# Layer 2's routed experts: the weights of a pair of experts laid side by side, loaded by three DMAs in place of six

## The reference, cut to what matters

```
g = jnp.einsum('ech,ehi->eci', buf, w_gate)
u = jnp.einsum('ech,ehi->eci', buf, w_up)
y = jnp.einsum('eci,eih->ech', jax.nn.silu(g) * u, w_down)
out_slots = y[flat_i, slot] * (flat_w * valid)[:, None]
```

## Time and profile before

| | us |
|---|---|
| median of 3 runs | 2361.2 |
| lowest and highest of them | 2356.06, 2362.68 |
| the profiled execution's time | 2355.61 |
| span of its trace, first to last instruction | 2353.9 |
| TensorE busy | 1996.5 (85%) |
| VectorE, GpSimd, ScalarE busy | 1291.5, 868.5, 757.3 |
| routed experts of layer 2, from about 1914 us on | some 440 |

### The profile page before, as it was taken

One profiled execution on the slowest core, in us unless ns is written; L12 is line 12 of the kernel. 1 busy time (PEld: TensorE's weight loads), 2 busy tenths in 40 slices (PEclk: granted clock), 3 DMA queues, 4 the chain that ended last, 5 costly groups with the idle time before them and its releaser, 6 DMA issues. The chain is left out here.

```text
span 2353.9 us, 39125 instructions
## 1 busy us (share of the span) xinstructions
PE 1996.5 (85%) x11898; PEld 1415.1 (60%) x11899; DVE 1291.5 (55%) x3013; ACT 757.3 (32%) x2192; POOL 868.5 (37%) x840
## 2 busy tenths in 40 slices
PE   1988888895699999569999999999999878878876
PEld 1666666663477777447777777777777643333332
DVE  5888888874244444336666777767666622111221
ACT  2323333322222222155544555554555211111110
POOL 5455665633343343142433333333343231211111
PEclk9998999997799999759999999999999989888898
DMA  6422222231133333422211111112222359999996
GB/s 214 153 84 89 88 73 89 86 120 41 45 100 103 104 97 101 145 71 83 78 64 65 64 65 63 65 64 77 96 82 80 105 188 351 357 356 351 361 358 183
DMA packets 129946, 315.30 MB, mean 134 GB/s; under 512 B 33346, under 2 KB 41538, under 8 KB 121604
## 3 DMA queue, kind: packets, MB, share of 16 engines
q1 hardware_dynamic: 102772, 260.64, 31.6%
q0 software_dynamic: 26880, 52.68, 7.8%
q10 hardware_dynamic: 144, 0.03, 0.0%
HBM read 253.13 MB, written 62.33 MB: 134 GB/s over the span
## 5 line engine op out<-in xcount | busy, mean ns | idle before, releaser
L1566 ACT ACTIVATE attn_pr<-attn_score_ps,attn_nmax 128x128 f32<-128x128 f32 x496 | 201.9, 419 | 198.7 <-DVE attn_nmax L1719 198.7
L1677 POOL DMA_INDIRECT list<-attn_pair,attn_pos x192 | 192.2, 1001 | 72.1 <-issue 61.1
L328 PE MATMUL attn_ffn_ps<-attn_xnT_high,attn_wgu_high 128*128 128x256 f32 x704 | 209.1, 297 | 9.2 <-DVE attn_hT_low L1811 8.2
L328 PE MATMUL attn_ffn_ps<-attn_xnT_low,attn_wgu_high 128*128 128x256 f32 x704 | 200.2, 284 | 0.0
L328 PE MATMUL attn_ffn_ps<-attn_xnT_high,attn_wgu_low 128*128 128x256 f32 x704 | 200.0, 284 | 0.0
L300 POOL TENSOR_SCALAR attn_norm_var_eps<-attn_norm_mean_var 128x2 f32<-128x2 f32 x32 | 7.9, 248 | 469.3 <-DVE attn_norm_mean_var L294 469.2
L1964 POOL DMA_INDIRECT out<-routed_ym,routed_place x32 | 50.2, 1569 | 340.9 <-DVE routed_ym L2127 267.4
L527 PE MATMUL wkv_ffn_ps<-wkv_xnT,wkv_wg 128*128 128x256 f32 x512 | 147.6, 439 | 24.9 <-DVE wkv_x L842 23.8
L1719 DVE TENSOR_REDUCE attn_nmax<-attn_score_ps 128x2 f32<-128x256 f32 x248 | 126.3, 551 | 60.2 <-PE attn_score_ps L1408 59.3
L1011 POOL DMA_INDIRECT y<-routed_ys,first_ffn_pair x72 | 74.0, 1028 | 230.3 <-DVE routed_ys L1161 230.3
L328 PE MATMUL routed_gu_ps<-routed_wgu_high,routed_xT_high 128*128 x288 | 126.0, 438 | 36.1 <-POOL first_ffn_wgu_low L968 36.1
(11 more groups left out here) (292 smaller groups left out, 5076.2 us busy)
## 6 DMA issues: line engine op xcount, KB each, us to landing
second_ffn_room<-in_w_gu SPq DMA_DIRECT2D x32, 1408.0 KB, 26.9
routed_wgu_a<-in_w_gu SPq DMA_DIRECT2D x16, 1408.0 KB, 24.4
routed_wgu_b<-in_w_gu SPq DMA_DIRECT2D x16, 1408.0 KB, 27.5
wkv_x<-in_x SPq DMA_DIRECT2D x32, 512.0 KB, 4.1
second_ffn_room<-y SPq DMA_DIRECT2D x32, 512.0 KB, 5.4
second_ffn_room<-in_w_down SPq DMA_DIRECT2D x32, 512.0 KB, 24.4
wkv_vT<-in_ctxT SPq DMA_DIRECT2D x16, 512.0 KB, 4.2
xn<-wkv_xn SPq DMA_DIRECT2D x16, 512.0 KB, 2.8
```

Source lines behind the costliest of these rows:

```text
L328: ins = nc.tensor.matmul(out, a[i], b[j], start=start and n == 0, stop=stop and n == 2)
L1566: nc.scalar.activation(pr[u % 2][:, a, j:2 * j + 1, :].rearrange("p k t -> p (k t)"), score_ps[:, a, KEYS[j]], ACT.Exp, bias=nmax[u % 2][: ...
L1677: nc.gpsimd.indirect_dma_start(io["list1"], bass.IndirectOffsetOnAxis(ap=pos[b.s][:, j, k:k + 1], axis=0), pair[b.s][:, j, k, :], None, bo ...
```

## The change

The weights of a pair are laid side by side in HBM, partition by partition, and in SBUF. A partition's share of gate and up of both experts is one run of 22,528 bytes, loaded by one DMA. Down is split by partitions and not by blocks: partitions 0 to 95 hold three rows of each expert, one run of 12,288 bytes, and partitions 96 to 127 hold two of each, 8,192 bytes in HBM that go to two places of 4,096 bytes in SBUF. That makes two DMAs, so a pair has three in place of six. The slots have the same size and number; SP's waits stand where they stood, and TensorE's counts are halved. The diff, without its repeated index changes:

```
-        wgu += [[m.sb(f"wgu_{s}_{z}", [P, 2, KC, H1]) for z in "ab"] for s in range(EARLY1, SLOTS1)]
-        wdn += [[m.sb(f"wdn_{s}_{z}", [P, HW, C]) for z in "ab"] for s in range(EARLY1, SLOTS1)]
+        wgu += [m.sb(f"wgu_{s}", [P, 2, 2, KC, H1])[:] for s in range(EARLY1, SLOTS1)]
+        wdn += [m.sb(f"wdn_{s}", [P, 2, HW, C])[:] for s in range(EARLY1, SLOTS1)]
...
-                        c.late.load_up(sp, io, 2 * q.i, slot, wgu[slot])
+                        c.late.load_up(sp, io, q.i, slot, wgu[slot])
...
-                    pe.wait_ge(up_in[q.s % SLOTS1], 32 * uses(q))
+                    pe.wait_ge(up_in[q.s % SLOTS1], 16 * uses(q))
...
-                    pe.wait_ge(down_in[q.s % SLOTS1], 64 * uses(q))
+                    pe.wait_ge(down_in[q.s % SLOTS1], 32 * uses(q))
...
-    def load_up(self, sp, io, e, slot, wgu):
-        for z in range(2):
-            sp.dma_start(wgu[z][:].rearrange("p z k n -> p (z k n)"), of(io, "w_gu1", e + z)).then_inc(self.up_in[slot], 16)
-
-    def load_down(self, sp, io, e, slot, wdn):
+        return self.at(s * self.SLOT + 4 * KC * H1, 2, -(-H1 // P), C)
+
+    def load_up(self, sp, io, q, slot, wgu):
+        sp.dma_start(wgu.rearrange("p e z k n -> p (e z k n)"), of(io, "w_gu1", q)).then_inc(self.up_in[slot], 16)
+
+    def load_down(self, sp, io, q, slot, wdn):
         full = H1 // P
-        for z in range(2):
-            sp.dma_start(wdn[z][:, 0:full, :].rearrange("p k n -> p (k n)"), of(io, "w_down1", e + z)).then_inc(self.down_in[slot], 16)
-            sp.dma_start(wdn[z][0:H1 - full * P, full, :], of(io, "w_down1_rest", e + z)).then_inc(self.down_in[slot], 16)
+        rest = H1 - full * P
+        sp.dma_start(wdn[0:rest].rearrange("p e k n -> p (e k n)"), of(io, "w_down1", q)).then_inc(self.down_in[slot], 16)
+        sp.dma_start(wdn[rest:, :, 0:full, :], of(io, "w_down1_rest", q).rearrange("p (e k n) -> p e k n", e=2, n=C)
+                     ).then_inc(self.down_in[slot], 16)
...
+    def by_pair(a):
+        return np.ascontiguousarray(a.reshape(PAIRS1, 2, a.shape[1], -1).swapaxes(1, 2)).reshape(PAIRS1, a.shape[1], -1)
+
...
+        "w_gu1": by_pair(np.stack([by_partition(i["L1_ffn_w_gate"]), by_partition(i["L1_ffn_w_up"])], axis=2)),
+        "w_down1": by_pair(np.concatenate([down1[:, :rest1], i["L1_ffn_w_down"][:, H1 // P * P:][:, :, None]], axis=2)),
+        "w_down1_rest": by_pair(down1[:, rest1:]),
```

More of the change, by code:

```diff
@@ L1347, in weights_ahead @@
                 def weights_ahead(s):
-                    c.late.load_up(sp, io, 2 * s, s, c.late.gate_up(s))
-                    c.late.load_down(sp, io, 2 * s, s, c.late.down(s))
+                    c.late.load_up(sp, io, s, s, c.late.gate_up(s))
+                    c.late.load_down(sp, io, s, s, c.late.down(s))
                 turns(sp, B, turn)
@@ L1946, in turn @@
                     if not isinstance(q.i, int) or q.i >= EARLY1:
-                        c.late.load_down(sp, io, 2 * q.i, slot, wdn[slot])
+                        c.late.load_down(sp, io, q.i, slot, wdn[slot])
                 rounds(sp, PAIRS1, turn, WAYS1)
@@ L1994, in projection @@
                         for z, half in enumerate(HALVES):
-                            ins = nc.tensor.matmul(bank[half, 0:H1], xT[q.s % 2][:, k, half], wgu[q.s % SLOTS1][z][:, n, k, :],
+                            ins = nc.tensor.matmul(bank[half, 0:H1], xT[q.s % 2][:, k, half], wgu[q.s % SLOTS1][:, z, n, k, :],
                                                    start=(k == 0), stop=(k == KC - 1))
@@ L2024, in down @@
                         for z, half in enumerate(HALVES):
-                            ins = nc.tensor.matmul(y_ps[half, :], hT[0:r, k, half], wdn[q.s % SLOTS1][z][0:r, k, :],
+                            ins = nc.tensor.matmul(y_ps[half, :], hT[0:r, k, half], wdn[q.s % SLOTS1][0:r, z, k, :],
                                                    start=(k == 0), stop=(k == HW - 1))
@@ L2209, in gate_up @@
     def gate_up(self, s):
-        return [self.at(s * self.SLOT + z * 2 * KC * H1, 2, KC, H1) for z in range(2)]
+        return self.at(s * self.SLOT, 2, 2, KC, H1)
     def down(self, s):
-        n = -(-H1 // P)
-        return [self.at(s * self.SLOT + 4 * KC * H1 + z * n * C, n, C) for z in range(2)]
-    def load_up(self, sp, io, e, slot, wgu):
-        for z in range(2):
-            sp.dma_start(wgu[z][:].rearrange("p z k n -> p (z k n)"), of(io, "w_gu1", e + z)).then_inc(self.up_in[slot], 16)
-    def load_down(self, sp, io, e, slot, wdn):
+        return self.at(s * self.SLOT + 4 * KC * H1, 2, -(-H1 // P), C)
+    def load_up(self, sp, io, q, slot, wgu):
+        sp.dma_start(wgu.rearrange("p e z k n -> p (e z k n)"), of(io, "w_gu1", q)).then_inc(self.up_in[slot], 16)
+    def load_down(self, sp, io, q, slot, wdn):
         full = H1 // P
-        for z in range(2):
-            sp.dma_start(wdn[z][:, 0:full, :].rearrange("p k n -> p (k n)"), of(io, "w_down1", e + z)).then_inc(self.down_in[slot], 16)
-            sp.dma_start(wdn[z][0:H1 - full * P, full, :], of(io, "w_down1_rest", e + z)).then_inc(self.down_in[slot], 16)
+        rest = H1 - full * P
+        sp.dma_start(wdn[0:rest].rearrange("p e k n -> p (e k n)"), of(io, "w_down1", q)).then_inc(self.down_in[slot], 16)
+        sp.dma_start(wdn[rest:, :, 0:full, :], of(io, "w_down1_rest", q).rearrange("p (e k n) -> p e k n", e=2, n=C)
+                     ).then_inc(self.down_in[slot], 16)
     def gather(self, nc, io, i):
@@ L2277, in by_partition @@
         return np.swapaxes(a.reshape(e, r // P, P, n), 1, 2)
+    def by_pair(a):
+        return np.ascontiguousarray(a.reshape(PAIRS1, 2, a.shape[1], -1).swapaxes(1, 2)).reshape(PAIRS1, a.shape[1], -1)
     i = {k: np.ascontiguousarray(v) for k, v in i.items()}
+    down1 = by_partition(i["L1_ffn_w_down"][:, :H1 // P * P])
+    rest1 = H1 % P
     return {
```

## The result

The changed kernel's four runs took 2429.42, 2456.03, 2474.5 and 2485.89 us (median 2465.27), the kernel before 2360.21 (4 runs, 2356.06 to 2362.68). It is slower, as forecast: by 83 us (59 to 106 by the interval) where 69 were summed.

The account below looks back on a forecast made before the run. The prediction took DMA transfers in layer 2's routed-expert stage as the bound: +2.5 for down's shape and -0.2 for packets gave +2.3 us a pair, +69 over 30 pairs, 2425 profiled, 2430 us as median. Range 2335 to 2465.

Parts of the forecast that it names:

- 69 were summed: Layer 2's routed experts: +2.5 - 0.2 = +2.3 us a pair, x 30 pairs, +69 us.
- The bound: Layer 2's routed experts: DMA transfers bound the stage, and what counts is how fast their bytes go.
- the signs that it named: Routed-expert stage: DMA share about 1.03, rate near 304 GB/s, gate and up near 425, down stretches under 240.
- Fewer, longer packets: Weight loads: 288 runs a pair in place of 704, 5 to 16 ns a packet, 0.2 us less a pair.
- Down's shape: Down's loads: all bytes go to 96 or 32 partitions, +2.5 us a pair, between 0 and +4.16.
- The 1.56 us: Down's loads before: 1.56 us a pair lost around 0.393 MB that go to 96 partitions.
- the by-the-byte end: Down's loads: if the loss comes by the narrow byte, 5.72 in place of 1.56, +4.16 us a pair.
- The port estimate: Down's loads: partitions 0 to 63 share eight of 16 ports, 4.81 us against 3.61, +1.2 a pair, 2391.
- Issues, waits, loads ahead, tail: 0: SP, TensorE, the two pairs loaded ahead and the stage's end: waits only change place, 0 us.
- Faster by packets and shape changes: Rival on down's loads: loss comes from many short packets and shape changes, and shrinks; 2332 or 2308; chance 0.21.
- The ceiling at 355 GB/s: Rival on the routed-expert stage: a ceiling near 355 GB/s holds, shape does not matter; same time, 2361; chance 0.07.
- Runs cut shorter: Rival on the weight loads: long runs are cut into shorter packets, the 0.2 is gone, 2436; no separate chance.

Follow-up runs that it names:

- the padded kernel: The change, with down's third block filled to 128 rows, so all weights go to 128 partitions in two long loads: 2312.24 us, ratio 0.982; again 2315.35.
- short runs: The change, with its load to 96 partitions cut into 2,048-byte runs: 2412.54 us, ratio 1.0228.
- the twins: Two-load kernel filled to 128 partitions, plus an unread load of 64 partitions x 6,144 bytes a pair: at 0 to 63 2429.92 us, at 32 to 95 2343.13.
- one wait more: The change, with SP issuing gate and up only when down of the pair two before has landed: 2452.53 us, ratio 1.0386.
- the first half of the change: Kernel before, with only gate and up laid side by side in 22,528-byte runs, down by its four loads: 2359.96 us, ratio 1.0021.
- the six short padded loads: Down filled up to 128 partitions, but loaded with gate and up in six loads of 11,264-, 4,096- and 2,048-byte runs: 2319.79 us, ratio 0.984.
- the padded ones with down alone: Two-load kernel filled to 128 partitions, with gate and up loaded per expert again, down in one long load: 2319.94 us, ratio 0.9828.

## Why the prediction was right, and what its terms missed

*The bound.* Right: DMA share 1.02, gate and up alone at 425, and the padded kernel shows that the time follows the rate. Of the signs that it named, the stage's rate is 283 GB/s where 304 were given, and the stretch with little but the narrow load ran at 264, not under 240; only the late mixed stretch did, at 234.

*Fewer, longer packets, -0.2 us a pair.* It failed here. In the padded shape the price of a packet holds (9 ns); beside narrow loads the paired gate and up gained nothing (stage +8 us, +0.27 a pair), and the long narrow packets cost. Length has one sign on 128 partitions and the other on 96. The prediction gave it one term with one sign; the other it had only as a clause under down's shape, on packets that "hold a busy place three times as long".

*Down's shape, +2.5.* Right in sign. The 1.56 us that it put on the narrow loads of before is nearly borne out: with the same six loads and down padded, the stage is 1.06 us a pair shorter although 131 KB more (0.31 us at 425 GB/s) move, 1.37 together. After the change, the profiled stages give down's shape 98 us, 3.3 a pair, nearer to the by-the-byte end of 4.16. But that end is not the reason: with short runs the bytes that go narrow cost 1.64 a pair, far less than 4.16, and the length of their packets adds up to 1.62. So the price is neither by the transfer (0) nor by the byte, and a second cause, the length, makes up the rest. For the first third of the stage the forecast was met: 309 GB/s where 304 was given, 15.5 us a pair for 15.85. What it lacked is that the pace would not stay: the engines drift apart and the pair rises to 19.3. The sum took one price for all 30 pairs. (Over the two runs of the change the whole loss is 2.8 us a pair, in the profiled one 3.5.)

*The port estimate, +1.2.* Too low, as the forecast judged; the twins agree with the placing behind it.

*Issues, waits, loads ahead, tail: 0.* Right. SP's wait moved to line 54 as said (406.2 us there), and one wait more left the stage as it was. The tail kept its length. Gathers and adds land after 19.0 and 16.5 us in place of 9.2 and 9.1, as allowed; the prediction did not say that GpSimd would then wait 412.7 us for its adds. The kernel with down alone paired has hardly any of that wait and is slower still.

*The rivals.* Faster by packets and shape changes: fell by the first half of the change (no gain) and the six short padded loads (the gain without longer runs). The ceiling at 355 GB/s: fell by 404. Runs cut shorter: fell, as the stage has 16,349 - 9,695 = 6,654 packets of 8 KB and more, near 30 x (128 + 96) = 6,720.

*The number.* 2430 against 2442.73: 13 us too low, and the 69 summed lie inside the interval of 59 to 106. On the profiled execution, for which the sum was made, 2425 stand against 2456. That it comes so near is partly luck: the size of +2.5 was a choice between two ends, neither of which holds, and one price for all pairs stood above the early pace and far under the late one. At 15.5 us for every pair the changed kernel would have taken (17.09 - 15.5) x 30 = 48 us less, which is under the forecast.

Left open: why the engines drift apart when narrow packets are long, why down's pairing costs more while gate and up stay short, and whether the 22,528-byte packets that stay quick beside a load to 0 to 63 are those to the other 64 partitions. The trace gives neither engine nor partition for a packet, so this was not followed further. A layout that needs no padding and leaves no load narrow was not tried.

## What to carry to other kernels

Look at which partitions a load goes to before its run lengths: in a stage bound by DMA, filling the last block up to 128 partitions gained 1.6% with the six loads of before and 1.8% with two, although it moves 3% more bytes, and merging loads by pair while leaving them narrow lost 3.5%. If a load has to be narrow, try 32 to 95 in place of 0 to 63, and keep its runs short. And price a shape by a stretch that holds it for many pairs: the first pairs of the changed stage, 1.9 us above the 13.6 of before, would have given a third of what the last ones cost, 5.7.

## What was not expected of the hardware

- A load to half the partitions costs its bytes (0.87 us a pair) or 4.6 times that (3.98), by which 64 they are.
- The slow load also slows its neighbours: the same 22,528-byte packets to all 128 partitions take 847 ns on the mean beside a load to partitions 32 to 95 and 1,032 beside one to 0 to 63; the DMA share reads 1.02 in both.
- With long narrow packets the 16 engines' shares of one load come apart by up to 27 us along the stage, with short ones by 7.5 and with no narrow load by 4; beside the load to partitions 0 to 63, in runs of 6,144 bytes, it is 18.
- Where all loads go to 128 partitions, the rows that GpSimd adds land the later the longer the packets of the other queue are: 8.6 us beside the six short padded loads, 10.3 and 11.5 beside the padded ones with down alone and both long. Down's narrow loads delay them as well: 14.2 with gate and up as before, 14.9 with short narrow runs, 16.5 beside the change's.

The Trainium skill (DMA: Bandwidth & Descriptors, "Rules for kernel authors") asks for 128 partitions and a MiB or more in one DMA. The padded kernel with two loads meets both. The change meets the size with two of its three loads (2,816 and 1,152 KB) and gives up the partitions for down, and is slower; the six short padded loads (1,408, 512 and 256 KB) keep the partitions, four of them under a MiB, and gain 1.6%. In this stage the partitions weigh more.
